# A gate table with 128 copies of its last row, one for each partition's out-of-range ids

## The reference

```python
x = emb_table[input_ids]                      # ids 2048 x 50
xp = einsum('bth,hk->btk', x, kernel) + b_i   # 384 values a token: z, r, h
for t in range(50):
    rec = h @ rec_kernel + b_r
    z = sigmoid(xz + rz); r = sigmoid(xr + rr)
    hh = tanh(xh + r * rh)
    h = z * h + (1 - z) * hh
logits = h_at(length - 1) @ emb_table.T       # 2048 x 12501
```

## Time and profile before

| | |
|---|---|
| three runs | 1506.21, 1494.87, 1493.6 us; median 1494.87 |
| the profiled execution | 1483.63 us, of which the profile's span is 1481.6 |
| mean granted TensorE clock in it | 0.897 |
| stages in the span | table to 83.7 us (first gather), first stage to about 676, second to about 1210, third to about 1402, last logits to the end |

### The profile page before, as it was taken

How to read it: one execution, slowest core, us unless ns; L and a number is a source line. 1 busy time by engine, 2 the same in 40 slices (tenths; PEclk the granted TensorE clock), 3 DMA queues, 4 the chain that set the end, 5 groups by cost and what they waited for, 6 DMA issues and landing times.

```text
span 1481.6 us, 21626 instructions
## 1 busy us (share of the span) xinstructions
PE 1150.9 (78%) x6340; PEld 933.7 (63%) x6340; DVE 905.3 (61%) x1684; ACT 690.5 (47%) x1203; POOL 820.2 (55%) x815
## 2 busy tenths in 40 slices
PE   7937767677677777767887878787787888888997
PEld 7825555555555555556765756666676677777875
DVE  7617666666666667667664655555475566566754
ACT  4513333333333333334554545454465467577743
POOL 0056666766766677666664555555465555455300
PEclk9978788888888888889898999999899999999999
DMA  9968799998979966867999999999998999999898
GB/s 317 344 163 139 146 139 141 137 157 137 143 154 138 143 149 145 150 141 133 182 214 198 215 186 217 194 217 192 186 261 201 235 196 243 220 273 246 247 358 320
DMA packets 127285, 293.22 MB, mean 198 GB/s; under 512 B 18080, under 2 KB 33312, under 8 KB 127264
## 3 DMA queue, kind: packets, MB, share of 16 engines
q0 software_dynamic: 51200, 157.34, 65.4%
q1 hardware_dynamic: 76064, 135.65, 24.9%
HBM read 171.30 MB, written 121.61 MB: 198 GB/s over the span
## 4 chain that ended last, share of the span: by engine, by line
PE 34%; DMA 19%; issue 17%; another core or an unknown queue 11%; DVE 10%; ACT 5%; POOL 3%; DVEq 0%; SPq 0%; ACTq 0%; POOLq 0%
DMA out_dram<-logits 10%; DMA gathered<-gate_table,index 7%; PE c_ps L393 4%; DVE c_ps L766 3%; PE r_ps L393 3%; POOL gathered L329 3%; PE r_ps L400 3%; PE x_ps L463 2%; PE x_ps L465 2%; PE x_ps L464 2%; PE c_ps L400 2%; PE c_ps L401 2%; PE r_ps L401 2%; PE z_ps L400 2%
## 5 line engine op out<-in xcount | busy, mean ns | idle before, releaser
L329 POOL DMA_INDIRECT gathered<-gate_table,index x800 | 816.5, 1021 | 570.2 <-PE c_ps L393 232.7
L766 DVE SCALAR_TENSOR_TENSOR c_ps<-c_ps,bias_sb,gates 128x512 f32<-128x512 f32 (+1 forms) x250 | 162.4, 650 | 239.0 <-ACT gates L565 189.2
L565 ACT ACTIVATE gates<-r_ps,zr_bias 128x512 f32<-128x512 f32 (+1 forms) x250 | 151.3, 605 | 297.1 <-remote 131.1
L393 PE MATMUL c_ps<-ident,gathered 128*128 128x128 f32 x800 | 115.6, 262 | 207.5 <-DVE c_ps L766 140.0
L393 PEld LDWEIGHTS c_ps<-ident,gathered 128*128 128x128 f32 x800 | 94.7, 149 | 275.7 <-DVE c_ps L766 172.0
L567 ACT ACTIVATE gates<-z_ps,zr_bias 128x512 f32<-128x512 f32 (+1 forms) x250 | 151.5, 606 | 209.4 <-remote 112.9
L775 DVE SCALAR_TENSOR_TENSOR gates<-gates 128x512 f32<-128x512 f32 (+1 forms) x250 | 146.7, 587 | 142.9 <-ACT gates L571 84.2
L589 ACT ACTIVATE logits<-x_ps,nan_row 128x512 f32<-128x512 f32 (+1 forms) x300 | 193.3, 680 | 84.4 <-DMA out_dram<-logits 48.0
L571 ACT ACTIVATE gates<-c_ps,bias_sb 128x512 f32<-128x512 f32 (+1 forms) x250 | 150.4, 602 | 101.1 <-PE c_ps L393 57.8
L771 DVE TENSOR_TENSOR kept<-gates,state 128x512 f32<-128x512 f32 (+1 forms) x250 | 145.0, 580 | 82.2 <-ACT gates L567 51.9
L393 PE MATMUL r_ps<-ident,gathered 128*128 128x128 f32 x800 | 117.4, 265 | 83.4 <-DMA gathered<-gate_table,index 62.9
(11 more groups left out here) (92 smaller groups left out, 1873.6 us busy)
## 6 DMA issues: line engine op xcount, KB each, us to landing
out_dram<-logits SPq DMA_DIRECT2D x192, 512.0 KB, 4.7
gate_table<-gates SPq DMA_DIRECT2D x24, 768.0 KB, 4.3
gathered<-gate_table,index POOLq DMA_INDIRECT x800
emb_rows<-in_L_rec_emb_table_dram SPq DMA_DIRECT2D x48, 256.0 KB, 4.6
out_dram<-logits SPq DMA_DIRECT2D x8, 213.0 KB, 4.0
logits<-in_r_input_ids_dram SPq DMA_DIRECT2D x1, 400.0 KB, 6.1
logits<-in_r_input_mask_dram SPq DMA_DIRECT2D x1, 400.0 KB, 6.7
w_in_sb<-in_L_rec_gru_kernel_dram SPq DMA_DIRECT2D x1, 192.0 KB, 2.5
```

Of the source, the lines that this page charges most:

```text
L329: nc.gpsimd.indirect_dma_start(gathered[:, q, n, :].bitcast(F32), None, table, bass.IndirectOffsetOnAxis(ap=index[:, g, n:n + 1], axis=0)) ...
L393: turned = nc.tensor.matmul(bank[:, n * P:(n + 1) * P].bitcast(F32R), gathered[:, q, n, gate * H:(gate + 1) * H], ident[:], is_transpose=T ...
L565: nc.scalar.activation(r_sb[:, b, 0:width], r_ps[:, b, 0:width], ACT.Sigmoid, bias=zr_bias[:, 1:2]).then_inc(s_r, 1)
L766: nc.vector.scalar_tensor_tensor(out=c_bank, in0=c_bank, scalar=bias_sb[:, 1, 2:3], in1=r, op0=ALU.add, op1=ALU.mult).then_inc(s_scaled, 1)
```

## The change

The table gets 128 rows between the last row and the freeze row, all copies of the last row: rows V to V + 127. One store on SP, issued behind the ragged rows, reads the last row from the one partition where it lies and writes it 128 times; POOL waits for it before the first gather. A number copy_f of p + 1 in partition p is made by an iota on POOL and a convert on DVE. For an id beyond V - 1 the row is now V - 1 + p + 1, where p is the partition, instead of V - 1; for that DVE has two more chained operations over 128 x 800. The freeze row is now row V + 128.

```diff
-    table = nc.dram_tensor("gate_table", [V + 1, G], F32).ap()
+    FREEZE = V + COPIES
+    table = nc.dram_tensor("gate_table", [FREEZE + 1, G], F32).ap()
...
-            sp.dma_start(table[V:V + 1, :], freeze_row).then_inc(s_freeze_out, 16)
+            sp.dma_start(table[FREEZE:FREEZE + 1, :], freeze_row).then_inc(s_freeze_out, 16)
...
             for j, m in RAGGED:
                 sp.dma_start(table[ragged_rows(j, m), :], table_rows[0:m, 0, j, :]).then_inc(s_table[0], 16)
+            j, m = RAGGED[-1]
+            last_row = table_rows[m - 1:m, 0, j, :].rearrange("p (a g) -> p a g", a=1)
+            sp.dma_start(table[V:V + COPIES, :].rearrange("(a n) g -> a n g", a=1),
+                         last_row.to_broadcast([1, COPIES, G])).then_inc(s_copies, 16)
...
+            nc.gpsimd.iota(copy_int[:], pattern=[[0, 1]], base=1, channel_multiplier=1).then_inc(s_iota, 1)
...
+            pool.wait_ge(s_copies, 16)
...
+                chained(nc.vector.tensor_copy(copy_f[:], copy_int[:]))
...
                 chained(nc.vector.tensor_tensor(row_f, row_f, flag_f, ALU.add))
+                chained(nc.vector.tensor_scalar(flag_f, row_f, float(V - 1), copy_f[:, 0:1], ALU.is_gt, ALU.mult))
                 chained(nc.vector.tensor_scalar(row_f, row_f, 0.0, float(V - 1), ALU.max, ALU.min))
+                chained(nc.vector.tensor_tensor(row_f, row_f, flag_f, ALU.add))
...
-                chained(nc.vector.scalar_tensor_tensor(out=rows, in0=flags, scalar=float(V), in1=numbers,
+                chained(nc.vector.scalar_tensor_tensor(out=rows, in0=flags, scalar=float(FREEZE), in1=numbers,
...
-MATH_STEPS = 15 + 3 + 4
+MATH_STEPS = 18 + 3 + 4
```

More of the change, by code:

```diff
@@ L19 @@
 HUGE = 3.0e38
+COPIES = 128
 def gru_logits(nc, ids, mask, emb, w_in, w_rec, bias, out):
@@ L131, in gru_logits @@
         bad = sb("bad", [P, NT])
+        copy_int = sb("copy_int", [P, 1], I32)
+        copy_f = sb("copy_f", [P, 1])
         z_sb, r_sb, cand = gates[:, 0], gates[:, 1], gates[:, 2]
@@ L164, in gru_logits @@
         s_freeze_out = sem("s_freeze_out")
+        s_copies = sem("s_copies")
         s_emb = [sem(f"s_emb{s}") for s in range(SLOTS)]
@@ L675, in last_positions @@
                 dve.wait_ge(s_ids, 32)
-                dve.wait_ge(s_iota, 1)
+                dve.wait_ge(s_iota, 2)
+                chained(nc.vector.tensor_copy(copy_f[:], copy_int[:]))
                 chained(nc.vector.tensor_reduce(length[:], mask_sb.rearrange("p (n t) -> p n t", t=T), AX.X, ALU.add))
```

## The result

The changed kernel takes 1420.03 us (median of 4 runs, 1417.11 to 1425.06); the kernel before, measured beside it, takes 1495.4 us. The ratio is 0.9487 with a 95% interval of 0.9441 to 0.9533: 75 us faster. The forecast was 1465 us with a range from 1422 to 1503, so the direction was right, the gain was more than twice the forecast one, and the time lies 2 us outside the range. The profiled execution took 1422.16 us, its span 1419.9. The profiled executions themselves differ by less, 61.5 us, because the one of before lies 12 us under its median.

What follows compares the result with a forecast made beforehand. The first stage was taken as bound by the recurrence through PE, ACT and DVE, with POOL a near second; later stages wait for gathers. Terms -24 - 10 - 2 + 4.5 + 1.7 = -30 us give 1465 us, range 1422 to 1503.

Steps and rivals of the forecast that it cites:

- (a): Gathers: DMA price falls to 10.6 engine-us each; first stage gains 0, later stages 24 us, bounds 0 and 63.
- I take half of 47.5, 24 us: Later stages: of 47.5 us idle before the r transposes that end with a gather, half comes back.
- (b): Logits stores in the later stages meet freer DMA engines, so PE waits less for ACT: 10 us gained, bounds 0 and 48.
- its 11 us: The profiled execution before the change lies 11 us under the median of the runs, 1494.87 us.
- (c): Start: POOL's first gather waits for the copies' store, 4.5 us lost; faster first gathers give 2 us back.
- (d): DVE's added convert and two chained operations in the table delay the start by 1.7 us, bounds 0 and 2.
- rival D: Slower through the copies' store at the start: 10.6 us more, 1505 us; sign: POOL's first gather over 92 us; chance 0.08.
- the three spread columns: First-stage columns 37, 38 and 40, gathering different rows: pace 11.5 to 12.3 us a column against 11.9, so no gain there.
- its weakest place: First stage: its largest waits are not named by the trace, so the forecast argued from three short columns.
- A: Waits change their names: time saved on gathers is waited for state, scaled candidate or ACT; 1486 to 1501 us; chance 0.18.
- C: 128 neighbouring rows meet in memory as one row does, so only the costs stay: 1501 us; chance 0.08.
- B: Full DMA queues also delay ACT and PE; first stage falls to POOL's pace, 65 us; 1370 to 1400 in all; chance 0.10.

Runs made afterwards that it cites:

- all_to_last: Changed kernel with copy number zero, so all ids beyond the table read the last row again, copies still stored; 1514.28 us, 1.0072 of the kernel before.
- before_half_stores: Kernel before the change, with the right half of each logits store of the second and third stage left out; 1469.82 us, ratio 0.9661.
- tile_of_copies: Changed kernel with its 128 copies projected as a third ragged tile and stored from 128 partitions; 1414.92 us, 0.9321 of the kernel before.
- one_gather: Changed kernel with only one of four gathers a block in the first stage, other rows zero; 1221.53 us, 0.8011 of the kernel before.
- copies16: Changed kernel with 16 copies instead of 128; 1255.03 us (0.8350 of the kernel before) on chip 7, 1418.94 us (0.9338) on chip 8.

## Why the prediction was right or wrong

**(a), price of a gather: right.** 10.6 engine-us were forecast, 10.9 came out over the whole span, and the queue's share of 38.4% lies within 35 to 45. all_to_last shows that the spreading does it.

**(a), later stages: the step that failed.** "I take half of 47.5, 24 us", because the state of two blocks before would be late next. What came back is 58.0 of 62.9 us, the part named "issue" too, and only 5.6 of it turned into other idle time of PE. The upper bound of 63 was thus nearly the answer, and the half was argued from code order, not from a row. The row that spoke was the DMA share of 0.93 and 0.98 in the earlier trace rows: the stages were held by the DMA engines' total work. before_half_stores shows this: relief on quite other bytes was worth 52 us, and nothing once the gathers were cheap. What is late next could have been read from PE's busy time: 429.93 x 0.93 + 167.93 x 0.98 = 564 us at full clock, far under the 726 us of the two windows, so there was room for the whole. (On chip 7 the same stages gave back far more, from 745 to 548 us.)

**A term that was missing.** The clock: PE's busy time in the later stages fell by 17.6 us for the same matmuls, as PE stood still less. The forecast read in the earlier trace rows that the clock rises with PE's busy share and charged nothing for it. With what was measured, 52.4 us less idle time of PE in place of (a)'s 24 and (b)'s 10, 17.6 for the clock and 6.95 for the start, the sum is 63 us, near the 61.7 by which the two profiled spans differ. The medians differ by 75; the rest is that the profiled execution of before is a fast one, which the prediction had allowed for by its 11 us.

**The range.** Its low end counts 63 us for (a) but 15 for (b), though (b)'s own bound was 48 and the sentence says that both bounds are in it. With 48 the low end would have been 1390, and 1420 inside.

**(b), logits stores: the mechanism on ACT was right, the gain was not there in this pair.** ACT's 48.1 us of waits for stores are gone, but PE's wait for ACT went from 15.0 to 16.1 us where 10 us of gain were taken. In before_half_stores it did fall, to 3.7, and on chip 9 from 21.2 to 15.5. What these matmuls still wait for ACT is thus in part not the stores' doing, and it moves between profiles; in this one the 10 us were too many by 10.

**(c) and (d), the start: mechanism right, the store under-sized.** DVE's part measured 2.2 us for 1.7 (1.75 in the pair on chip 9), within what this issue moves from run to run. The store with its issue cost 6.45 us for 4.5, the first gathers gave 1.7 back for 2. Together PE starts 6.95 us later, where 4.2 were forecast. The landing of 9.2 us against 2.5 for a load of the same size over 128 partitions fits a store bound to its one partition, and tile_of_copies shows that this is 6 us (3.3 us of landing). The Trainium skill, "SBUF — State Buffer", section "Door 1: The DMA port swizzle", has 27.6 GB/s for one port, by which, as an estimate, the bytes take 7.1 us; the trace agrees roughly, with 6.45 us of cost, and 7.1 would have been the better term than 4.5. POOL's first gather at 92.31 us is over the 92 that was set as rival D's mark; all_to_last measured D's price, 10.4 us, but its condition, that (a) and (b) give less than 4 us, didn't hold in the change itself.

**The first stage: the number was right by luck, the reason wrong.** "The stage does not notice" held in the result (607.6 to 612.3 us with the same 50 columns), as the three spread columns had told; on chip 7 it would have failed by 62 us. But "bound elsewhere: by the recurrence through PE, ACT and DVE" fell: one_gather runs the same recurrence in 405 us. What falls away there with three gathers in four is ACT's 200 us of waits named "remote", the ones that the forecast had called its weakest place.

**The rivals.** A fell: before "c_ps <- DVE" PE's idle time in the later stages is 41.6 and 6.8 us after, 40.5 and 3.6 before; DVE's idle time before `kept` grew from 20.0 to 44.1 us, and it did not reach PE. C fell with the queue's share, 38.4% at the same bytes, and all_to_last (69.4%) shows that it is the spreading that lowers it. B's mechanism fell too: full DMA queues were to be what delays PE and ACT under the names "remote" and "issue", but ACT's "remote" in the first stage stayed (212.7 and 217.3 us) when the DMA share went from 0.86 to 0.50, and stayed at 0.21 (192.3). On chip 7 B's number came out, a first stage of 532 us for 530, yet by another way: all_to_last has no "remote" wait there and 149.7 us of named waits for gathers, which spread rows brought down to 97.1. The forecast knew one chip. The change itself gained 5.1 to 6.8% on the chips where it ran; on chip 7 it did not run, and its sibling with 16 copies gained 16.5%.

## What to carry to other kernels

Where many partitions of a gather read one and the same row of memory, give it a second copy and send neighbouring partitions to different ones; two copies did here what 128 did. When a stage's DMA share is near one, do not discount the waits for transfers in it without a row that says so (58.0 of 62.9 us came back here), and add what the clock gives back. Add up the waits that the trace names "remote" before calling a stage bound by its recurrence: here that was 213 us of 608, and one kernel with fewer gathers showed that the recurrence needs 405. Measure a gain on more than one chip.

## What was not expected of the hardware

- Equal rows in a gather of 128 x 1536 B cost about twice the DMA time (20.6 against 10.6 engine-us), and two copies of the row, alternating by partition, are enough to lose that: the queue's share with 2, 16 and 128 copies is 41.6, 44.3 and 38.4% of spans of 1406, 1252 and 1420 us, 11.7, 11.1 and 10.9 engine-us a gather.
- POOL's gathers slow a stage in which nobody is seen to wait for them: 608 us with four a block, 608.6 with a third of the bytes, 405 with one, 407.4 with one and a higher DMA share (0.60) than with four (0.50). The time shows as some 200 us of ACT's waits named "remote", 2.3 us with one gather. On chip 7 these waits are absent with four gathers as well. The cause stays open.
- The same program differs between chips by 12%: 1255.03 and 1418.94 us for copies16, while the kernel before differs by 1% (1503.87 and 1519.26). Each chip ran one group of kernels at one time, so chip and occasion are not told apart, and the cause stays open.
